# Router logits as 16 more columns of the mixing product, and expert choices ahead of the second norm of groups 1 and 2, in a one-core Perceiver layer

## The chip, the core and the metric

The kernel runs on one core of a Trainium2 chip. A core has five engines with queues of their own: PE (TensorE, matmul), DVE (VectorE), ACT (ScalarE), POOL (GpSimd) and SP (SyncE, which here issues DMAs only). Each engine works through its own list in order and waits on semaphores that the others raise. The metric is device time in microseconds of one execution, the median of several runs. All data are fp32 except where the text says otherwise; an fp32 matmul of 128 columns appears in the trace as two PE instructions.

## What is computed

32 batches of 32 query rows with 128 features (1024 tokens) pass through three residual blocks. Cut to what matters:

```python
x = x + xattn(layernorm(x), ctx, ctx, ...)            # 16 heads of 8, 257 keys per batch
# second block, u = layernorm(x), per batch of 32 rows
xf = concat([u[:, :1], u[:, 1:] @ WB.T]); xb = concat([u[:, 1:] @ WBf.T, u[:, -1:]])
gamma = sigmoid(xf @ w1.T + xb @ w2.T + b)            # one number per token
x = x + gamma * (xf + xb) + (1 - gamma) * u
# third block, v = layernorm(x): 8 experts, 2 per token
weights, chosen = top_k(v @ gate_kernel, 2); weights = softmax(weights)
x = x + sum over the 2 chosen of weight * ((silu(v @ w0[e]) * (v @ w1[e])) @ wo[e])
```

## The kernel before

Tokens stand on partitions in NT = 8 tiles of 128, and in three groups of tiles: group 0 is tiles 0 to 2, group 1 tiles 3 to 5, group 2 tiles 6 and 7 (`GROUPS`). There are three stages.

**Attention** is a loop over the 32 batches. Per batch PE makes keys and values (L843, L845), scores (L864), transposed probabilities (L876) and the weighted values (`weigh_values`, L905); DVE takes the row maxima, ACT the exponentials. In the batches 1 to 12 a query step of a later tile stands ahead of L905 (`late_step`, L899 and L902), and DVE's `take_output` drains it. POOL adds the heads of each batch (`add_heads`).

**The tail and the mix.** The output projection (`output_product`) and `add_residual` give x1. For each group: `row_sums` and `variances` on DVE (bn_stats, bn_aggr), an inverse root and a shift on POOL (`inverse_roots`), a normalisation on ACT (groups 0 and 1) or DVE (group 2), PE's transposes (`turn`), the shifted copies z, first and end (`shifted_features`), and then `mix`, with four matmuls per tile: z times `mix_sb[0]`, z one row on times `mix_sb[1]`, the first rows times w1, the last rows times an identity. Their output has D + 1 = 129 columns: 128 for the mixed rows less u, and one for the argument of gamma. The two vectors for that column of `mix_sb` come from `mix_vectors` (L920, L921) at the end of the attention loop. `gates` on ACT makes gamma; `mixed_rows` on DVE makes x2 = gamma * mixed + (u + x1).

**The experts.** x2 is normalised again by the same steps (`normalise(2, ...)`), transposed, and multiplied by the gate kernel (`logits`, L947). DVE's `best` and `best_at` find the two best of 8 per token; `pick` and `chosen` (L1419, L1422) are one-hots of them. PE counts the tokens of each expert and ranks them (L1017 to L1023). The rows are sent to `table` in DRAM by SP (L389, after the weights of both choices are in, `top_w_ready`), and 23 slots of 128 rows, each of one expert, are gathered back from it by POOL (`gather`, L590), transposed (`turn_slots`, L1069), and run through the expert (`half_hidden`, L1082; `project`, L1093). The first two slots (experts 0 and 1) don't wait for the table: one-hot matrices `late_at` are made on POOL, ACT and DVE from `early_rank`, and PE multiplies the normalised rows by them (`early_product`, L1031). `name_slots` (L1061) finds the row numbers for the gathers; `slot_row` (L1489) is what POOL waits for. ACT loads its Silu table (L735) after the weights.

The order is written out by hand in every engine's block. `keep_clock_up` (L805) is a matmul whose result nobody reads; it stands once ahead of the first turn and twice between the turns and the logits. `keep_sum` (L1009) moves x2 into two banks for the final sum.

Of the kernel before, what the change touches and what calls it, by code (L numbers as in the profile page):

```python
# [45 lines left out]
NT = TOK // 128  # L46
# [27 lines left out]
FAR = 4096  # L74

# [6 lines left out]
def build(nc, x, ctx_keys, ctx_last, weights, mix_back, vectors, rows, gate, w01, wo, out):  # L82
    with ExitStack() as stack:
# [3 lines left out]
        def sem(name):  # L87
# [50 lines left out]
        mix_sb = sb("mix_sb", [128, 2, D + 1])  # L138
        end_sb = sb("end_sb", [128, D + 1])
        u_x1 = sb("u_x1", [128, NT, D])  # L140
        gamma = sb("gamma", [128, NT])
# [57 lines left out]
        planes = nc.dram_tensor("planes", (TOPK * TOK, D), F32).ap()  # L199
        table = nc.dram_tensor("table", (TABLE_ROWS + 1, ROW), F32).ap()  # L200
# [52 lines left out]
        normed, norm_turned, norm_ft_ready, z_ready, edges_ready = (  # L253
            [sem(f"{name}{g}") for g in range(len(GROUPS))]
            for name in ("normed", "norm_turned", "norm_ft_ready", "z_ready", "edges_ready"))
        kl_done, kl_ready, wo_done = sem("kl_done"), sem("kl_ready"), sem("wo_done")
        mix_in, mix_ready, vectors_done, mixed_done, gamma_ready, u_x1_ready = (
            sem(n) for n in ("mix_in", "mix_ready", "vectors_done", "mixed_done", "gamma_ready", "u_x1_ready"))
        last_rows_ready = sem("last_rows_ready")
        logits_done, top_ready, top_w_ready, chosen_ready, ranks_done = (  # L260
            sem(n) for n in ("logits_done", "top_ready", "top_w_ready", "chosen_ready", "ranks_done"))
# [4 lines left out]
        first_gather_in, empty_stored = sem("first_gather_in"), sem("empty_stored")  # L266
        early_rank_ready, apart_ready = (sem(n) for n in ("early_rank_ready", "apart_ready"))
        pool_at_ready, act_at_ready = ([sem(f"{name}{n}") for n in range(EARLY)] for name in ("pool_at_ready", "act_at_ready"))
        dve_at_ready = sem("dve_at_ready")
# [38 lines left out]
        turn1_bank, turn2_bank = (bank[0], bank[1], bank[4]), (bank[3], bank[0], bank[1])  # L308
        logits_bank = (bank[2], bank[3], bank[0])
        ranks = bank[7][:, 192:192 + NT * E]  # L310
# [5 lines left out]
        def mixed(g, t):  # L316

            return mixed_bank[g][:, (D + 1) * t:(D + 1) * (t + 1)]
# [20 lines left out]
        def _(sp):  # L339
# [10 lines left out]
            sp.dma_start(table[TABLE_ROWS:TABLE_ROWS + 1, :], empty_row[0:1, :]).then_inc(empty_stored, 16)  # L350
            sp.wait_ge(zero_ready, 1)
# [31 lines left out]
            for g in range(len(GROUPS)):  # L383
                for c in range(TOPK):
                    if c == 1:
# [20 lines left out]
        def _(pool):  # L406
# [8 lines left out]
            def inverse_roots(nth):  # L415

                for g in range(len(GROUPS)):
                    t = group_tiles(g)
                    pool.wait_ge(var_ready, len(GROUPS) * (nth - 1) + g + 1)
                    if g < len(GROUPS) - 1:  # L420
                        own(pool.tensor_tensor(rstd[:, t], var_eps[:, t], minus_half[:, t], ALU.pow))
                        pool.tensor_tensor(shift[:, t], minus_mean[:, t], rstd[:, t], ALU.mult).then_inc(shift_ready, 1)
                    else:
                        pool.tensor_tensor(rstd[:, t], var_eps[:, t], minus_half[:, t], ALU.pow).then_inc(rstd_ready, 1)
# [30 lines left out]
            def expert_constants():  # L455
# [22 lines left out]
                pool.iota(no_row[:], [[0, 1]], base=TABLE_ROWS, channel_multiplier=0).then_inc(consts_ready, 1)  # L478
# [5 lines left out]
                pool.memset(ones[:], 1.0).then_inc(consts_ready, 1)  # L484
                own(pool.memset(before[:], 1.0))
# [6 lines left out]
            def mix_constants(m):  # L492

                if m == 0:
                    pool.memset(z_ft[:], 0.0).then_inc(mix_ready, 1)
# [5 lines left out]
                else:  # L501
                    pool.memset(end_ft[:], 0.0)
                    pool.tensor_copy(mix_sb[:, 1, 0:D], w_sb[:, W_BF]).then_inc(mix_ready, 1)

# [50 lines left out]
            for b in range(B + 2):  # L555
# [6 lines left out]
                if b >= 2:  # L562
                    add_heads(b - 2)
# [4 lines left out]
                if b % BPT == 2 and 2 <= b // BPT < 5:  # L568
                    mix_constants(b // BPT - 2)
# [3 lines left out]
            inverse_roots(1)  # L573
# [6 lines left out]
            inverse_roots(2)  # L580

            pool.wait_ge(normed[2], 2)
            for g in range(len(GROUPS)):
                t = group_tiles(g)
                pool.wait_ge(normed[g], 2)
                pool.tensor_copy(rows_tok[:, t, 1, 0:D], rows_tok[:, t, 0, 0:D]).then_inc(twin_ready, 1)
# [6 lines left out]


            pool.wait_ge(consts_ready, 13)
            pool.wait_ge(empty_stored, 16)
            pool.indirect_dma_start(slot_sb[SLOT_BUFS - 1][:], None, table, bass.IndirectOffsetOnAxis(no_row[:], 0)
                                    ).then_inc(first_gather_in, 16)

            pool.wait_ge(early_rank_ready, 1)  # L600
            for s in range(EARLY):
                for t in range(HT if s == 0 else 1):
                    pool.tensor_scalar(late_at[s][:, t, :], far_slot_nos[:], early_rank[:, t, s:s + 1], None, ALU.is_equal
                                       ).then_inc(pool_at_ready[s], 1)
# [3 lines left out]
            pool.wait_ge(first_gather_in, 16)  # L608
            for s in (2, 0, 3, 1, 4, 5):
# [23 lines left out]
        def _(act):  # L633
# [17 lines left out]
            def gates(g):  # L651

                act.wait_ge(mixed_done, g + 1)
                columns = mixed_bank[g][:, 0:(D + 1) * len(group(g))].rearrange("p (t c) -> p t c", c=D + 1)[:, :, D]
                act.activation(gamma[:, group_tiles(g)], columns, ACT.Sigmoid, bias=vec_sb[:, V_B]).then_inc(gamma_ready, 1)

            def features(g):

                act.wait_ge(norm_turned[g], 2)
                act.activation(norm_ft[:, group_tokens(g)], turn2_bank[g][:, group_columns(g)], ACT.Copy  # L660
                               ).then_inc(norm_ft_ready[g], 1)

# [61 lines left out]
            features(0)  # L724
            normalise(2, 1, x2_tok, rows_tok[:, :, 0, 0:D])
            features(1)

            for g in range(len(GROUPS)):
                act.wait_ge(top_ready, g + 1)
                for c in range(TOPK):  # L730
                    act.activation(rows_tok[:, group_tiles(g), c, D], top_d[:, group_tiles(g)], ACT.Sigmoid,
                                   scale=1.0 - 2.0 * c).then_inc(top_w_ready, 1)


            act.activation(table_loader[:], minus_half[:, 0:1], ACT.Silu)  # L735

# [5 lines left out]
            def early_at(s, t):  # L742

                act.wait_ge(apart_ready, HT * s + t - HT + 1)
# [3 lines left out]
            def early_one_hots(s):  # L748

                early_apart(s, HT)  # L750
                for t in range(HT, NT):
# [30 lines left out]
            early_one_hots(0)  # L782
            slot_features(0)
            early_one_hots(1)
# [15 lines left out]
        def _(pe):  # L800
# [87 lines left out]
            def weigh_values(b):  # L888
# [11 lines left out]
                elif step == "queries":  # L900
                    pe.wait_ge(late_ft_ready, i - LATE_TILES[0] + 1)
                    pe.matmul(o_bank[:, 384:512], w_sb[:, W_Q], norm_ft[:, tile(i)], start=True, stop=True)  # L902
                for g in range(G):
# [13 lines left out]
            def mix_vectors():  # L917

                pe.wait_ge(mix_in, 16)
                pe.matmul(bank[6][:, 384:385], mix_back_sb[:, 0, :], vec_sb[:, V_W1], start=True, stop=True)  # L920
# [680 lines left out]
```

## Time and profile before

| | us |
|---|---|
| median of 3 runs (lowest, highest) | 221.71 (221.41, 222.21) |
| the profiled execution | 223.38 |
| its span, first to last instruction | 221.6 |
| busy: PE, DVE, ACT, POOL | 207.0, 151.0, 139.1, 125.4 |
| granted TensorE clock, mean | 0.994 |

The granted clock is told as a share of full speed; its two levels are 2.4 GHz (1.0) and 1.2 GHz (0.5). The profile's chain of waits follows the work that ended last back from release to release; PE holds 79% of it, DVE 7%. In time it has three parts: up to about 113 us the attention loop, to about 141 us the tail, the mix, the second norm and the choices, and from there the 23 slots.

### The profile page before, as it was taken

Reading aid. Unit: us, or ns where it says so; the run is one execution under the profiler, and the core shown is the slowest. Engines: PE = TensorE matmul, PEld = TensorE weight load, DVE = VectorE, ACT = ScalarE, POOL = GpSimd, SP = SyncE. Lnnn points to the kernel's source line nnn. Section 1 sums busy time; section 2 is a strip of 40 time slices with the busy share of each in tenths; the row PEclk is TensorE's granted clock in tenths of the full one; section 3 lists DMA queues with packets and bytes.
Section 4 is the critical chain, followed back from the end, with each engine's and each line's share of the span. In section 5 each row is a group of like instructions: output and inputs, shape, how many; then the busy total and the mean of one; then the engine's idle time right before and its main releaser. Section 6 shows DMA issues by size and latency. Waiting matters only on the chain.

```text
span 221.6 us, 6244 instructions
## 1 busy us (share of the span) xinstructions
PE 207.0 (93%) x2069; PEld 176.3 (80%) x2069; DVE 151.0 (68%) x508; ACT 139.1 (63%) x436; POOL 125.4 (57%) x229
## 2 busy tenths in 40 slices
PE   6989999999999999999997889799999999999981
PEld 6866877887877777777775686589999999999970
DVE  3598887888787786878767577874445565655812
ACT  2158988988888988998895635753224444444300
POOL 2695575556675464353225547527777777775322
PEclk9999999999999999999999999999999999999997
DMA  6868406052160670000000001802122211122053
GB/s 185 304 211 304 154 19 237 10 173 78 30 224 15 220 215 12 7 12 4 13 5 3 3 0 52 158 11 50 51 54 56 48 42 46 38 44 40 6 189 95
DMA packets 14865, 18.93 MB, mean 85 GB/s; under 512 B 3039, under 2 KB 10467, under 8 KB 14834
## 3 DMA queue, kind: packets, MB, share of 16 engines
q1 hardware_dynamic: 12962, 15.35, 21.6%
q0 software_dynamic: 1440, 2.65, 5.8%
q10 hardware_dynamic: 432, 0.54, 0.7%
q8 instruction: 17, 0.28, 0.5%
q14 instruction: 14, 0.11, 0.2%
HBM read 14.73 MB, written 4.13 MB: 85 GB/s over the span
## 4 chain that ended last, share of the span: by engine, by line
PE 79%; DVE 7%; DMA 4%; POOL 3%; ACT 2%; issue 2%; POOLq 1%; SPq 1%; DVEq 0%; ACTq 0%
PE bank L1082 18%; PE bank L876 12%; PE bank L864 9%; PE bank L843 9%; PE bank L1093 8%; PE bank L905 8%; PE bank L845 6%; PE bank L1031 2%; DMA pt_sb<-planes 2%; DMA x_tok<-x 2%; DVE neg_max L1254 1%; PE bank L1069 1%; DMA planes<-y_sb,y_row 1%; POOL u_x L579 1%; PE bank L805 1%
## 5 line engine op out<-in xcount | busy, mean ns | idle before, releaser
L695 ACT ACTIVATE p_sb<-bank,neg_max 128x257 f32<-128x257 f32 x128 | 59.0, 473 | 15.3 <-DVE neg_max L1254 15.3
L1254 DVE TENSOR_REDUCE neg_max<-bank 128x1 f32<-128x257 f32 x128 | 46.0, 417 | 6.2 <-PE bank L864 5.7
L537 POOL TENSOR_TENSOR o_half<-o_masked 128x64 f32<-128x64 f32 x32 | 10.2, 318 | 45.8 <-DVE o_masked L1279 45.8
L704 ACT ACTIVATE pt_sb<-bank 128x512 f32<-128x512 f32 x64 | 35.0, 611 | 0.3 <-PE bank L876 0.3
L876 PE MATMUL bank<-ident,p_sb 128*128 128x128 f32 x256 | 33.3, 273 | 0.2 <-ACT pt_sb L704 0.2
L1082 PE MATMUL bank<-slot_ft,w_now 128*128 128x128 f32 x240 | 30.9, 276 | 0.0
L1551 DVE TENSOR_TENSOR hid_ft<-silu_sb,bank 128x512 f32<-128x512 f32 x23 | 15.8, 688 | 20.2 <-PE bank L1082 13.0
L876 PEld LDWEIGHTS bank<-ident,p_sb 128*128 128x128 f32 x256 | 28.9, 141 | 0.7 <-issue 0.7
L1082 PEld LDWEIGHTS bank<-slot_ft,w_now 128*128 128x128 f32 x240 | 29.1, 192 | 0.1
L590 POOL DMA_INDIRECT slot_sb<-table,slot_row x23 | 22.6, 984 | 10.7 <-issue 9.2
L616 POOL DMA_INDIRECT planes<-y_sb,y_row x21 | 22.2, 1059 | 10.5 <-DVE y_sb L1532 5.0
L771 ACT ACTIVATE slot_ft<-bank 128x128 f32<-128x128 f32 x23 | 6.4, 277 | 33.0 <-PE bank L1069 30.5
L695 ACT ACTIVATION_READ_ACCUMULATOR p_sb<-bank,neg_max 128x1 f32 x128 | 25.9, 203 | 0.0
L864 PE MATMUL bank<-kv_sb,qbd_sb 32*128 32x257 f32 x256 | 24.1, 429 | 1.3 <-DVE kv_sb L1264 1.3
L1093 PE MATMUL bank<-wo_sb,hid_ft 128*128 (+1 forms) x184 | 24.3, 275 | 0.0
L843 PE MATMUL bank<-ctx_sb,w_sb 128*128 128x256 f32 x64 | 22.7, 437 | 0.0
L1093 PEld LDWEIGHTS bank<-wo_sb,hid_ft 128*128 128x128 f32 x184 | 22.4, 192 | 0.0
L905 PE MATMUL bank<-pt_sb,kv_sb 128*32 128x128 f32 x512 | 21.3, 279 | 0.0
L845 PEld LDWEIGHTS bank<-w_sb,ctx_sb 128*128 128x128 f32 x128 | 19.8, 196 | 1.8
L1264 DVE TENSOR_TENSOR kv_sb<-bank,kv_bias 128x512 f32<-128x512 f32 x31 | 21.1, 682 | 0.0
L845 PE MATMUL bank<-w_sb,ctx_sb 128*128 128x128 f32 x128 | 19.9, 279 | 0.0
L516 POOL TENSOR_TENSOR ctx_sb<-ctx_sb,last_sb 128x256 f32<-128x256 f32 x31 | 18.9, 614 | 0.1
(219 smaller groups left out, 337.7 us busy)
## 6 DMA issues: line engine op xcount, KB each, us to landing
w_sb<-w SPq DMA_DIRECT2D x8, 512.0 KB, 4.8
ctx_sb<-ctx_keys SPq DMA_DIRECT2D x7, 512.0 KB, 4.1
wo_sb<-wo SPq DMA_DIRECT2D x8, 256.0 KB, 5.1
planes<-zero_rows SPq DMA_DIRECT2D x2, 512.0 KB, 6.6
pt_sb<-planes SPq DMA_DIRECT2D x4, 256.0 KB, 3.6
table<-rows_tok SPq DMA_DIRECT2D x4, 195.0 KB, 4.2
out<-norm_tok SPq DMA_DIRECT2D x2, 256.0 KB, 2.3
x_tok<-x SPq DMA_DIRECT2D x1, 448.0 KB, 5.0
```

The lines of the kernel that those rows point to most:

```text
L590: pool.indirect_dma_start(slot_sb[s % SLOT_BUFS][:], None, table, bass.IndirectOffsetOnAxis(slot_row[:, s:s + 1], 0)).then_inc(slot_in[s % ...
L616: pool.indirect_dma_start(planes, bass.IndirectOffsetOnAxis(y_row[s % Y_BUFS][:], 0), y_sb[s % Y_BUFS][:], None, bounds_check=last_row, oo ...
L695: act.activation(p_sb[b % 2][:, g, :], s_bank[g][:, 0:SKV], ACT.Exp, bias=neg_max[b % 2][:, g:g + 1], accum_out=sums[:, b, g:g + 1]).then_ ...
L704: act.activation(pt_sb[b % 2][:, t, :], pt_bank[t][:], ACT.Copy).then_inc((pt0_ready, pt1_ready)[t], 1)
L843: pe.matmul(kv_bank[:, 0:KEYS], w_sb[:, W_K], ctx[:, k, :], start=True, stop=True)
L845: last = pe.matmul(kv_bank[:, KEYS + 128 * t:KEYS + 128 * (t + 1)], ctx[:, k, tile(t)], w_sb[:, W_V], start=True, stop=True)
L864: pe.matmul(s_bank[g][:, 0:SKV], qbd_sb[b // BPT % 2][rows, b % BPT, :, :].rearrange("p j q -> p (j q)"), kv_sb[b % KV_BUFS][rows, 0, :], ...
L876: last = pe.transpose(pt_bank[t][:, tile(g)], p_sb[b % 2][:, g, tile(t)], ident[:])
L905: last = pe.matmul(o_bank[SQ * g:SQ * (g + 1), 0:128], kv_sb[b % KV_BUFS][:, 1, 128 * t + SQ * g:128 * t + SQ * (g + 1)], pt_sb[b % 2][:, ...
L1082: last = pe.matmul(bank[2 * m + s % 2][:, tile(c)], weights_now[:, tile(c)], slot_ft[s % 2][:], start=True, stop=True)
L1093: last = pe.matmul(bank[5][:, 0:D], hid_ft[s % 2][:, c, :], rows, start=(c == 0), stop=(c == FC - 1))
L1254: dve.tensor_reduce(neg_max[b % 2][:, g:g + 1], s_bank[g][:, 0:SKV], AX.X, ALU.max, negate=True).then_inc(max_ready, 1)
```

## The change

The mixing product gets 16 more columns (`COLS` = 145), from which the router's logits follow without the second norm's rows. The gate kernel less its column means, `centred`, is made once: PE multiplies the gate kernel by a matrix of 1/128 in batch 14 of the attention loop, DVE subtracts. In batch 18 PE multiplies WB and WBf by `gate_w` (the gamma vector beside `centred`), which replaces `mix_vectors`; POOL fills the constant parts in batch 22 (`mix_constants(3)`). Of the 16 columns 8 carry the logits of xf + xb - u and 8 those of u; DVE's `best` multiplies them by gamma and by 1 + std (`coef`; `deviations` on POOL), adds the two, and takes the best 8. Since the second norm's scale is one positive number per token, the choice needs no scale; `scale_tops` on POOL multiplies the difference of the two best by rstd before ACT makes the weights. Gone are `mix_vectors`, `features`, `logits`, the second `turn` and all three `keep_clock_up`.

```diff
-            keep_clock_up(1, bank[5])
             turn(1, 0, norm_tok, turn1_bank[0])
             pe.wait_ge(mix_ready, 5)
+            pe.wait_ge(vectors_ready, 1)
             mix(0, range(0, 2))
...
-            turn(2, 0, rows, turn2_bank[0])
...
+            pe.wait_ge(x2_ready, 2)
             keep_sum(0)
-            keep_sum(1)
             pe.wait_ge(chosen_ready, 1)
...
+            pe.wait_ge(x2_ready, 3)
+            keep_sum(1)
...
+                pe.wait_ge(normed[0], 2)
+                pe.wait_ge(normed[1], 2)
+                pe.wait_ge(dve_at_ready[0], 1)
+                for t in range(2, HT + 1):
+                    early_product(0, t, t == 2, False)
...
+                elif b == CENTRED_AT:
...
+                    pe.matmul(o_bank[:, 384:384 + E], mean_mat[:], gate_sb[:], start=True, stop=True)
+                elif b == VECTORS_AT:
...
+                        pe.matmul(o_bank[:, 384 + 16 * m:384 + 16 * m + 1 + E], mix_back_sb[:, m, :], gate_w[:, m, :],
+                                  start=True, stop=True)
...
+                own(dve.tensor_tensor(logit_parts[:, t, :, :],
+                                      mixed_tiles(g)[:, :, D + 1:COLS].rearrange("p t (k e) -> p t k e", e=E),
+                                      coef[:, t, :].unsqueeze(3).to_broadcast(by_part), ALU.mult))
+                own(dve.tensor_tensor(router[:, t, :], logit_parts[:, t, 0, :], logit_parts[:, t, 1, :], ALU.add))
...
+            best(0)
+            mixed_rows(0)
+            row_sums(0, x2_tok)
             best_at(0)
-            features(2)
+            variances(0)
             best(1)
+            mixed_rows(1)
+            best_at(1)
             best(2)
...
+            mixed_rows(2)
+            row_sums(1, x2_tok)
...
+            early_one_hots(0, 2)
+            variances(1)
+            row_sums(2, x2_tok)
+            variances(2)
```

Other moves: the last batch's heads are added on DVE in one reduction (`add_last_heads`) instead of on POOL, and `variances(0)` of the first norm stands ahead of the last `take_output`; `variances(1)` stands ahead of `add_residual(2)`. On POOL the first indirect DMA (a dummy gather, now from a table of its own, `first_table`) stands ahead of the second norm's roots, and the copies of the rows for choice 1 (`twin`) of groups 1 and 2 stand behind all one-hots. SP sends the rows of choice 0 after `normed` and those of choice 1 after `twin`. ACT makes the weights of groups 1 and 2 and loads the Silu table behind the one-hots.

On DVE, before, the choices end the second norm's list (`bank3` and `bank0` hold the logits of groups 1 and 2):

```order
L1188 COPY norm_ft<-bank1 128x256 [waits norm_turned2]
L1393 MAX top<-bank3 128x8 [waits logits_done]
L1393 MAX top<-bank3 128x8 x2
L1395 TENSOR_TENSOR top_d<-top 128x3 [waits dve_step]
L1393 MAX top<-bank0 128x8 [waits logits_done]
L1393 MAX top<-bank0 128x8
L1395 TENSOR_TENSOR top_d<-top 128x2 [waits dve_step]
L1401 MAX_INDEX top_at<-top,bank3 128x8 x3
L1401 MAX_INDEX top_at<-top,bank0 128x8 x2
L1419 TENSOR_TENSOR pick<-expert_no,top_at 128x64 [waits consts_ready,dve_step]
L1419 TENSOR_TENSOR pick<-expert_no,top_at 128x64
L1422 TENSOR_TENSOR chosen<-pick 128x64 [waits dve_step]
```

Now, from the choices of group 2 on, the x2 rows of group 2 and the statistics of group 1 come behind `chosen`:

```order
L1457 MAX_INDEX top_at<-top,router 128x8 [waits tops_ready]
L1457 MAX_INDEX top_at<-top,router 128x8
L1473 TENSOR_TENSOR pick<-expert_no,top_at 128x64 [waits consts_ready,dve_step]
L1473 TENSOR_TENSOR pick<-expert_no,top_at 128x64
L1476 TENSOR_TENSOR chosen<-pick 128x64 [waits dve_step]
L1392 SCALAR_TENSOR_TENSOR x2_tok<-bank7,coef,u_x1 128x128 [waits u_x1_ready,gamma_ready]
L1392 SCALAR_TENSOR_TENSOR x2_tok<-bank7,coef,u_x1 128x128
L1195 BN_STATS stats<-x2_tok 128x6 [waits x2_ready]
L1195 BN_STATS stats<-x2_tok 128x6 x2
L1500 SCALAR_TENSOR_TENSOR early_rank<-chosen,bank5 128x16 [waits ranks_done]
L1486 TENSOR_TENSOR z_ft<-far_slot_nos,early_rank 128x384 [waits early_rank_ready]
L1203 BN_AGGR mean_var<-stats 128x2 [waits dve_step]
```

So the choice no longer waits for any normalised row, and the variance of group 1 waits for the choice. On PE, before, the ranks are followed by the early products, which wait only for one-hots:

```order
L1023 MATMUL bank7<-chosen,ones 128x16
L1023 MATMUL bank7<-chosen,ones 128x8
L1031 MATMUL bank3<-z_ft,rows_tok 128x128 [waits pool_at_ready0,expert_in]
L1031 MATMUL bank3<-z_ft,rows_tok 128x128 [waits act_at_ready0]
L1031 MATMUL bank3<-z_ft,rows_tok 128x128 [waits pool_at_ready0]
```

Now the second half of x2 is moved behind the ranks, and the early products wait for normalised rows too:

```order
L1055 MATMUL bank5<-chosen,ones 128x16
L1055 MATMUL bank5<-chosen,ones 128x8
L1041 MATMUL bank6<-x2_tok,ident 128x512 [waits x2_ready]
L1065 MATMUL bank3<-z_ft,rows_tok 128x128 [waits normed1,dve_at_ready0,normed0,expert_in]
L1065 MATMUL bank3<-z_ft,rows_tok 128x128 x2
L1065 MATMUL bank3<-z_ft,rows_tok 128x128 [waits pool_at_ready0]
L1065 MATMUL bank3<-z_ft,rows_tok 128x128 [waits act_at_ready0]
```

Between the mix and `normed1` PE is left with two moves of x2 and the ranks.

## Rows read from the trace of the kernel before

**Rows 1.** Chain of waits, attention: start us, us, engine, line, instructions.

```profile
60.34 0.22 PE bank L902 x2
```

**Rows 2.** Timeline of PE, last batch: start us, us, engine, line, work [idle before].

```profile
116.16 1.06 PE L876 MATMUL bank<-ident,p_sb 128*128 128x128 f32 x8 [0.17 <-ACT pt_sb L704]
```

**Rows 3.** Timeline, first norm of group 0 on DVE, POOL and ACT.

```profile
118.13 0.67 DVE L1153 BATCH_NORM_STATS2 stats<-x_tok 128x6 f32<-128x128 f32 x3
...
120.35 0.89 POOL L421 TENSOR_TENSOR rstd<-var_eps,minus_half 128x3 f32<-128x3 f32 x1
...
121.55 1.26 ACT L638 ACTIVATE norm_tok<-x_tok,shift,rstd 128x128 f32<-128x128 f32 x3 [2.12 <-POOL shift L422]
```

**Rows 4.** Timeline of PE, the mix; each tile starts with L932.

```profile
124.07 0.68 PE L932 MATMUL bank<-mix_sb,z_ft 128*128 128x129 f32 x4 [0.66 <-ACT z_ft L647]
...
127.37 0.61 PE L932 MATMUL bank<-mix_sb,z_ft 128*128 128x129 f32 x4
...
128.27 0.61 PE L932 MATMUL bank<-mix_sb,z_ft 128*128 128x129 f32 x4
```

**Rows 5.** Chain of waits, second norm of group 0.

```profile
127.87 0.88 DVE x_tok L1337 x3
...
128.77 0.69 DVE stats L1153 x3
...
129.49 0.32 DVE mean_var L1161 x3
...
130.15 0.87 POOL rstd L421
...
131.32 1.27 ACT rows_tok L638 x3
```

**Rows 6.** Chain of waits, choices, and early products of slot tile 1.

```profile
138.22 0.81 DVE top_at L1401 x6
...
139.45 0.23 DVE chosen L1422
...
146.67 1.90 PE bank L1031 x16
```

**Rows 7.** Timeline of PE, early products of slot tile 0.

```profile
141.38 2.48 PE L1031 MATMUL bank<-z_ft,rows_tok 128*128 128x128 f32 x16 [1.09 <-POOL z_ft L603]
```

**Rows 8.** Timeline of DVE: in the list of ranks, and behind it.

```profile
141.06 0.21 DVE L1445 TENSOR_TENSOR square<-n_tiles,expert_before 128x64 f32<-128x64 f32 x1
...
145.89 0.54 DVE L1485 TENSOR_TENSOR late_at<-far_slot_nos,early_rank 128x384 f32<-128x384 f32 x1
```

**Rows 9.** Timeline of POOL, its one-hots of slot tile 0.

```profile
140.62 2.48 POOL L603 TENSOR_SCALAR z_ft<-far_slot_nos,early_rank 128x128 f32<-128x128 f32 x4 [2.03 <-DVE early_rank L1435]
```

**Rows 10.** Timeline of ACT, Silu table and first steps of its one-hots.

```profile
138.66 1.28 ACT L735 ACT_TABLE_LOAD   x1
...
140.60 0.69 ACT L739 ACTIVATE z_ft<-far_slot_nos,early_rank 128x128 f32<-128x128 f32 x2 [0.44 <-DVE early_rank L1435]
```

**Rows 11.** Timeline of POOL, the first gather.

```profile
147.66 1.04 POOL L590 DMA_INDIRECT slot_sb<-table,slot_row  x1 [3.98 <-issue]
```

**Rows 12.** Chain of waits, PE takes slot 2.

```profile
150.97 0.11 PE bank L1069
```

**Rows 13.** DMA issues, 130 to 160 us: KB each, median us from issue to landing.

```profile
table<-rows_tok SPq DMA_DIRECT2D x2, 130.0 KB, 5.7
slot_sb<-table,slot_row POOLq DMA_INDIRECT x8, 2.5
```

**Rows 14.** Timeline of PE at the start of the span.

```profile
1.75 4.64 PE L817 MATMUL bank<-ident 128*128 128x128 f32 x20 [1.75 <-POOL ident L445]
...
9.65 1.06 PE L817 MATMUL bank<-ident 128*128 128x128 f32 x4
```

**Rows 15.** Timeline of PE, its last work.

```profile
214.66 2.02 PE L1103 MATMUL bank<-y_sb,late_at 128*128 128x128 f32 x16 [0.54 <-DVE y_sb L1532]
```

**Rows 16.** Busy by window: window, length, PE, PEld, DVE, ACT, POOL busy, PEclk, DMA.

```profile
219.00:219.50 0.50, 0.00 (x0) 0.00 (x0) 0.00 (x0) 0.00 (x0) 0.00 (x0) 0.60 0.26 76
```

More of the change, by code:

```diff
@@ L571, in _ @@
                     residual(2 * (b // BPT - 2) + b % BPT // 3)
-            inverse_roots(1)
+            for g in range(len(GROUPS)):
+                inverse_root(1, g)
+            deviations()
             pool.wait_ge(normed[2], 1)
@@ L653, in gates, with top_weights @@
                 act.wait_ge(mixed_done, g + 1)
[L654 to L661, printed above, removed]
+                act.activation(coef[:, group_tiles(g), 0], mixed_tiles(g)[:, :, D], ACT.Sigmoid, bias=vec_sb[:, V_B]
+                               ).then_inc(gamma_ready, 1)
+            def top_weights(g):
+                act.wait_ge(top_ready, g + 1)
+                for c in range(TOPK):
+                    act.activation(rows_tok[:, group_tiles(g), c, D], top_d[:, group_tiles(g)], ACT.Sigmoid,
+                                   scale=1.0 - 2.0 * c).then_inc(top_w_ready, 1)
             act.dma_start(w_sb[:], weights).then_inc(w_in, 16)
@@ L723, in _ @@
             gates(2)
[L724 to L735, printed above, removed]
+            top_weights(0)
             def early_apart(s, t):
@@ L781, in _ @@
             act.wait_ge(early_rank_ready, 1)
-            early_one_hots(0)
+            early_one_hots(0, HT + 1)
+            normalise(2, 1, x2_tok, rows_tok[:, :, 0, 0:D])
+            top_weights(1)
+            top_weights(2)
             slot_features(0)
-            early_one_hots(1)
+            early_one_hots(1, HT)
+            act.activation(table_loader[:], minus_half[:, 0:1], ACT.Silu)
             gate_silu(0)
@@ L941, in mix @@
                     last.then_inc(mixed_done, 1)
-            def logits(g):
-                pe.wait_ge(norm_ft_ready[g], 1)
-                for n, t in enumerate(group(g)):
-                    last = pe.matmul(logits_bank[g][:, E * n:E * (n + 1)], norm_ft[:, tile(t)], gate_sb[:],
-                                     start=True, stop=True)
-                last.then_inc(logits_done, 1)
             pe.wait_ge(consts_ready, 1)
@@ L1016, in _ @@
             for t in range(NT):
-                last = pe.matmul(bank[7][:, 128:128 + E], ones[:], chosen[:, t, :], start=(t == 0),
+                last = pe.matmul(counts, ones[:], chosen[:, t, :], start=(t == 0),
                                  stop=(t == NT - 1))
@@ L1336, in mixed_rows @@
                 for n, t in enumerate(group(g)):
[L1337 removed]
+                    last = dve.scalar_tensor_tensor(out=x2_tok[:, t, :], in0=mixed(g, n)[:, 0:D], scalar=coef[:, t, 0:1],
                                                     in1=u_x1[:, t, :], op0=ALU.mult, op1=ALU.add)
```

243 lines of the change are left out of this document (148 added, 95 removed).

## The prediction

> **What bounds the kernel now.** I read four views in this order. The chain of waits shows which engine has no slack where. In the attention loop it is PE alone, piece behind piece without a gap: even a query product that one batch more or less carries stands on the chain with its full 0.22 us [rows 1]. From about 113 us on, the chain changes engine every half microsecond: norm, mix, norm again, choices. From the early products at 141.38 on [rows 7] it is PE again, to the end. The timelines of the single engines then show what each wait is for, the DMA issues when the table is readable, and the windows the granted clock. So three things can be gained or lost: PE work in the loop, the length of the path from the last batch to the early products, and the level of PE's clock. All positions below are on the scale of the trace of before, whose span is 221.6 us; the program's own time was 223.38, so 1.8 lie around the span and stay. I add the differences to the median, 221.71.
>
> **Attention: +0.6.** Three small products join PE's list in batches 14 and 18. As the loop has no gap, each counts. The row shows 0.22 for one of 128 columns [rows 1]; these have 8 or 9 columns but load as many weights, so I take 0.2 each, 0.6, with 0.3 and 0.66 as ends. The two products that they replace stood where PE waited for ACT's copy anyway, 0.17 idle even with them in front [rows 2]: their removal gives nothing.
>
> **First norm: -0.9.** The row sums of group 0 end at 118.80, yet POOL begins the root at 120.35 only [rows 3]: the statistics stood behind the last drain, and POOL behind the last heads. Now the statistics follow the sums at once. From first aggregate to root takes 0.66 (129.49 to 130.15 [rows 5]), so the root can start at 119.46, 0.9 earlier. ACT's normalisation, PE's turn and the mix start (124.07 [rows 4]) follow by the same 0.9, since the unread 512-column product ahead of that turn is gone as well. Adding the last heads on DVE costs one reduction there and saves two POOL steps: nothing net. I keep -0.7 to -1.0.
>
> **Mix: +0.08 a tile.** A tile takes 0.90 (127.37 to 128.27 [rows 4]) for four matmuls, three of them 129 columns wide, so some 0.224 per matmul. 16 columns more are an eighth: 0.028 for each of the wide three, nothing for the fourth, which goes from 1 to 17. That makes 0.08 a tile, between 0 and 0.11. Group 0 is mixed 0.65 earlier (three tiles), all eight 0.25 earlier, at about 131.7.
>
> **Choices: 4.6 earlier.** DVE takes group 0 at 127.87 - 0.65 = 127.2. `best(0)` is two small dependent steps, as `chosen` 0.23 each, and three maxima, as the index steps 0.135 each (0.81 for six [rows 6]): 0.86. Then x2 0.88, sums 0.69 [rows 5], indices 0.41, statistics 0.66: POOL's root starts at 130.7, 0.55 later than before. It is 1.17 from there to ACT (130.15 to 131.32) and 1.27 through it [rows 5]: 133.15. The gate of group 2 stands behind that in ACT's queue, another quarter microsecond by estimate from the small steps: 133.4. `best(2)` 0.73, two indices 0.27, and 0.65 for `pick` and `chosen` (139.03 to 139.68 [rows 6]) give `chosen` at 135.05, against 139.68.
>
> **Second norm: most of that is given back.** The early products now wait for the normalised rows of group 1, and these for statistics behind `chosen` on DVE: x2 of group 2 (0.59), sums (0.69), rank 0.2, one-hots 0.54 [rows 8], statistics 0.66 put POOL's root at 137.75; 1.17 and 1.27 more, and a handover of 0.1, put the first product at 140.3. Before: 141.38 [rows 7]. So 1.1 is left of 4.6. The products themselves took 2.48 there, since they waited for POOL's and ACT's one-hots; with these ready they take 1.90, as those of slot tile 1 do [rows 6]. End: 142.2 instead of 143.87, 1.7 earlier. Behind them DVE's list limits: sums and statistics of group 2 end it at 138.75, then the 5.4 from early rank to 145.89 [rows 8] and 0.6 for normalising group 2, so 144.75, 1.15 earlier; PE needs only the second half of it there, and comes out 1.5 to 1.6 earlier at slot tile 1. POOL's one-hot for the sixth product (0.62 [rows 9]) ends 0.5 before its turn. The Silu load, 1.28 and once hidden, now stands behind eight one-hot steps of 0.3 [rows 10] and ahead of `slot_features(1)`; ACT gets free 0.1 to 0.2 before it is needed. I price that at 0, up to 0.5. Total of the path: **-1.5**.
>
> **Gathers: 0.** Slot 2 was gathered from 147.66 [rows 11], landed 2.5 later [rows 13] and was taken at 150.97 [rows 12]: 0.8 of slack. `slot_row` moves by about as much as PE. The last table rows go out at about 142.5 now, behind two one-hots and two row copies on POOL; before, the last two needed 5.7 [rows 13], with six stores close together and the dummy gather among them. Four stand together now and the gather is far ahead; I take 3 and no cost.
>
> **The clock: +1.6.** This term decides the sign. Between the end of the mix (131.7) and the first early product (140.3) PE has two moves of x2 of 0.9 each and the ranks, 0.6: 2.4 us of work in 8.6. The second move starts when x2 of group 2 is there, at 135.65, and ends at 136.55; then PE has nothing for 3.7 us. The unread products that stood in this stretch are gone. In the trace of before the longest pause of PE between the loop and the end of the slots is the 1.09 us ahead of these products [rows 7], and the granted clock is full there. It falls once: PE's last work ends at 216.68 [rows 15], the window from 219.0 reads 0.60 [rows 16], so the clock went from 2.4 to 1.2 GHz at about 219.1, after 2.4 us without work. An idle stretch of 3.7 us, behind a thin one, is more of the same. What the lower level costs is seen at the start: 20 instructions of 128 columns in 4.64 [rows 14] are 0.44 per product with the last one's tail off, against 0.24 [rows 6], so 0.2 more each. If the eight early products run at it, that is **1.6**. Nearest below is 0 (no fall). Above, the start shows PE still at the lower level in the products at 9.65 [rows 14], 8 us after its first work; at the same pace here `half_hidden(0)` with its eight matmuls would pay another 1.6, and the next early products some more. I take the eight products, the value between.
>
> **Sum.** 221.71 + 0.6 - 1.5 + 1.6 = **222.4**, slower by 0.3%, which is also about the smallest difference that a measurement of this kernel can tell from none.
>
> **Rivals.** *The clock stays high* (chance 0.30): same sum without the last term, 220.8, so 0.4% faster. For it: the stretch isn't empty, and the moves of x2 are the densest work there. Against it: 3.7 us of nothing. It decides by whether PE's clock falls before 140.3. *The clock stays low for longer, or falls a second time* (0.20): after the last batch PE has, without the first unread product, only about 1 us of work between 119.7 and 123.1; if the clock is low in the mix too, or through `half_hidden(0)`, another 1.6 is paid: 224.0. *The table lands late* (0.08): with 5.7 again the last rows land at 148.2, the gather starts then and lands at 150.7, while PE wants slot 2 at 149.5, so 1.2 to 2 lost, 222 to 222.8 with a high clock. A rule speaks for this one: the Trainium skill, SBUF — State Buffer, § Who interferes with whom, says that GpSimd and a VectorE operation with two SBUF inputs lock each other out for a whole instruction, and `twin` of groups 1 and 2 now runs beside DVE's long one-hots. The row beside it speaks against: DVE's two-input step at 141.06 took its 0.21 [rows 8] in the middle of POOL's four one-hots at 0.62 each [rows 9]. By the rule the stores would leave a microsecond later, by the row at once. *The change doesn't do what it says* is not left: the choices wait for no normalised row in the new order; what can fail is only that their lead is worth little, which the sum has in it.
>
> **How the numbers follow.** Forecast 0.42, clock high 0.30, clock low for longer 0.20, late table 0.08. The limits of 0.3% are 221.05 and 222.37. Faster: three quarters of the high clock, 0.24 with a rest. Same: what is left of it, nearly half of the forecast, a part of the late table: 0.28. Slower: 0.48. The range has to hold the high clock at -0.3 for the uncertain terms, 220.5, and the long fall, 224.1.
>
> **What would show it.** Right: a PEclk under 1 between 137 and 146 us of the new trace, early products of over 0.3 per product, `chosen` at about 135.7 (0.6 later on the new scale), first early product near 140.9, batches 14 and 18 longer by 0.2 and 0.4. Wrong: a clock of 1 throughout; PE waiting for slot 2; ACT's table load ahead of `slot_features(1)` on the chain; PE idle for less than 3 us ahead of the early products.

## The result, and the profile after

The changed kernel takes **224.79 us** (median of 20 runs, 222.19 to 227.07) where the kernel before took 221.50 in the same comparison (20 runs, 220.67 to 222.21): ratio 1.013, 95% interval 1.011 to 1.015, so 3.3 us slower. Medians are of all runs; ratios and intervals, here and below, leave out runs over 1.5% above the fastest of their kernel, three of the twenty here. The forecast had the sign, but only 0.7 us of it (222.4 on its base of 221.71), and the time lies above its range, which ended at 224.1.

First a correction to the scale. The trace of before took 223.38 us, 1.9 over its median, and the difference lies wholly at its start, which the change doesn't touch: by their durations PE's first products ran at the lower level until past 10 us [rows 14]. Another trace of the kernel before (run e10 below, 221.96 us) has an early start, as that of after has, and everything behind it stands 1.9 us earlier than in the rows ahead of the prediction. Rows of after are therefore compared with those of e10. From PE's timeline in e10 (start, duration, line, in brackets the idle time before and who ended it):

```profile
11.94 1.06 PE L864 MATMUL bank<-kv_sb,qbd_sb 32*128 32x257 f32 x8 [0.88 <-DVE kv_sb L1264]
...
114.25 1.06 PE L876 MATMUL bank<-ident,p_sb 128*128 128x128 f32 x8 [0.17 <-ACT pt_sb L704]
...
119.81 1.02 PE L805 MATMUL bank<-w_sb,ident 128*128 128x512 f32 x2
...
122.16 0.68 PE L932 MATMUL bank<-mix_sb,z_ft 128*128 128x129 f32 x4 [0.66 <-ACT z_ft L647]
...
139.47 2.48 PE L1031 MATMUL bank<-z_ft,rows_tok 128*128 128x128 f32 x16 [1.09 <-POOL z_ft L603]
...
147.00 2.05 PE L1082 MATMUL bank<-slot_ft,w_sb 128*128 128x128 f32 x16 [0.37 <-ACT slot_ft L771]
148.89 0.27 PE L1069 MATMUL bank<-ident,slot_sb 128*128 128x128 f32 x1
...
212.77 2.02 PE L1103 MATMUL bank<-y_sb,late_at 128*128 128x128 f32 x16 [0.54 <-DVE y_sb L1532]
```

The same timeline of after (the rows answer to [rows 2, 4, 6, 7, 12, 15]):

```profile
11.88 1.07 PE L914 MATMUL bank<-kv_sb,qbd_sb 32*128 32x257 f32 x8 [0.88 <-DVE kv_sb L1301]
...
114.67 1.06 PE L926 MATMUL bank<-ident,p_sb 128*128 128x128 f32 x8 [0.62 <-ACT pt_sb L762]
...
119.79 0.71 PE L975 MATMUL bank<-w_sb,att_ft 128*128 128x128 f32 x4 [1.13 <-DVE att_ft L1366]
120.51 0.78 PE L861 MATMUL bank<-ident,norm_tok 128*128 128x128 f32 x3
121.95 1.30 PE L986 MATMUL bank<-mix_sb,z_ft 128*128 128x145 f32 x4 [0.66 <-ACT z_ft L705]
...
123.96 1.17 PE L986 MATMUL bank<-mix_sb,z_ft 128*128 128x145 f32 x4
...
128.17 0.66 PE L986 MATMUL bank<-mix_sb,z_ft 128*128 128x145 f32 x4
...
129.14 0.66 PE L986 MATMUL bank<-mix_sb,z_ft 128*128 128x145 f32 x4
...
136.35 0.35 PE L1049 MATMUL bank<-chosen,ones 128*128 128x8 bf16 x8 [1.93 <-DVE chosen L1476]
...
136.86 1.23 PE L1041 MATMUL bank<-x_tok,ident 128*128 128x512 f32 x2
141.50 3.49 PE L1065 MATMUL bank<-z_ft,rows_tok 128*128 128x128 f32 x16 [3.41 <-ACT rows_tok L696]
...
150.05 2.05 PE L1124 MATMUL bank<-slot_ft,w_sb 128*128 128x128 f32 x16 [0.37 <-ACT slot_ft L817]
151.94 0.27 PE L1111 MATMUL bank<-ident,slot_sb 128*128 128x128 f32 x1
...
216.07 2.02 PE L1145 MATMUL bank<-y_sb,late_at 128*128 128x128 f32 x16 [0.54 <-DVE y_sb L1601]
```

The mix begins 0.2 earlier than in e10, yet its first tile takes 2.01 (121.95 to 123.96) where a later one takes 0.97 (128.17 to 129.14), and the early products take 3.49. The windows of after say why (the last number but two is the granted clock):

```profile
120.00:122.00 2.00, 1.33 (x8) 0.77 (x7) 1.86 (x12) 1.09 (x5) 0.89 (x2) 0.67 0.00 0
122.00:124.00 2.00, 2.00 (x9) 2.00 (x10) 0.85 (x5) 1.26 (x3) 1.62 (x5) 0.50 0.00 0
124.00:126.00 2.00, 2.00 (x10) 1.99 (x10) 0.00 (x0) 0.00 (x0) 2.00 (x3) 0.50 0.00 0
126.00:128.00 2.00, 2.00 (x13) 2.00 (x12) 0.57 (x3) 0.64 (x3) 1.67 (x2) 0.62 0.00 0
128.00:130.00 2.00, 2.00 (x18) 2.00 (x19) 1.26 (x8) 0.26 (x1) 0.00 (x0) 1.00 0.31 33
...
136.00:138.00 2.00, 1.65 (x18) 0.77 (x18) 1.90 (x9) 0.04 (x1) 0.29 (x1) 0.94 0.50 149
138.00:140.00 2.00, 0.09 (x1) 0.00 (x0) 1.90 (x15) 1.84 (x7) 1.80 (x4) 0.50 0.01 4
140.00:142.00 2.00, 0.50 (x2) 0.53 (x3) 1.94 (x13) 1.75 (x7) 1.84 (x6) 0.50 0.00 0
142.00:144.00 2.00, 2.00 (x12) 2.00 (x11) 1.97 (x7) 0.00 (x0) 2.00 (x4) 0.50 0.33 100
144.00:146.00 2.00, 1.63 (x11) 1.44 (x11) 2.00 (x3) 0.97 (x4) 0.93 (x1) 0.85 0.65 186
```

PE's clock falls to 1.2 GHz twice: from about 120.7 to 127.5 us, under the mix of group 0, and from about 137.8 to 144.6, under the early products. The forecast had the second fall alone, and read it from the pause of 3.41 us ahead of the early products. The rows put it earlier: at 137.8 PE is still at the second move of x2 (136.86 to 138.09), behind a pause of 1.93, and the long pause has not begun.

### The profile page after: what moved, and what is told of

It is laid out like the page before. It is cut to its first block, busy times and chain, and to the rows that moved or that the text cites. A ratio compares the mean times of both kernels' runs of the same rounds, so it can differ in the third digit from the quotient of the medians.

```text
span 223.0 us, 6218 instructions
## 1 busy us (share of the span) xinstructions
PE 204.0 (92%) x2041; PEld 175.4 (79%) x2041; DVE 151.9 (68%) x515; ACT 137.5 (62%) x432; POOL 127.6 (57%) x243
## 4 chain that ended last, share of the span: by engine, by line
PE 78%; DVE 9%; DMA 4%; ACT 3%; issue 2%; POOL 1%; POOLq 1%; SPq 1%; DVEq 0%; ACTq 0%
PE bank L1124 17%; PE bank L926 12%; PE bank L914 9%; PE bank L893 8%; PE bank L966 8%; PE bank L1135 8%; PE bank L895 6%; PE bank L1065 2%; DMA pt_sb<-planes 2%; DMA x_tok<-x 2%; PE bank L986 1%; DVE neg_max L1291 1%; ACT rows_tok L696 1%; PE bank L1111 1%; DMA planes<-y_sb,y_row 1%
## 5 line engine op out<-in xcount | busy, mean ns | idle before, releaser
L674 POOL DMA_INDIRECT planes<-y_sb,y_row x21 | 21.6, 1030 | 11.3 <-DVE y_sb L1601 5.9
L895 PEld LDWEIGHTS bank<-w_sb,ctx_sb 128*128 128x128 f32 x128 | 19.3, 191 | 1.7
L895 PE MATMUL bank<-w_sb,ctx_sb 128*128 128x128 f32 x128 | 19.4, 274 | 0.0
```

The lines of the kernel that those rows point to most:

```text
L674: pool.indirect_dma_start(planes, bass.IndirectOffsetOnAxis(y_row[s % Y_BUFS][:], 0), y_sb[s % Y_BUFS][:], None, bounds_check=last_row, oo ...
L895: last = pe.matmul(kv_bank[:, KEYS + 128 * t:KEYS + 128 * (t + 1)], ctx[:, k, tile(t)], w_sb[:, W_V], start=True, stop=True)
```

## The experiments

The theory drawn from these rows: the path gets shorter as forecast, and two falls of the clock eat that and more. The rivals: the longer mix and the new order themselves cost; the table comes late. Each run has its median, its lowest and highest time, and the ratio to the kernel before, timed beside it (221.67 for e1 to e4, 221.57 for e5 to e7), with a 95% interval.

**e1, the mix filled.** One unread product is put back, in a place where PE waits anyway.

```diff
             spread_last()
+            keep_clock_up(1, bank[5])
             output_product(2)
```

> The changed kernel (224.8 us, median of its runs) with one product that nobody reads put back, between `spread_last()` and `output_product(2)`, where PE sat idle for 1.13 us. Clock theory: the change's loss comes from two stretches in which PE's granted clock is 0.50, the first from about 121 to 127 us of the changed kernel, in the mix of group 0, because the unread product that stood ahead of that mix is gone. In that stretch the two turns and the three mix tiles of group 0 took about 3.0 us more than at the upper level (tiles of 2.01, 1.88 and 1.26 us against 0.97, turns of 0.78 and 1.07 against 0.55). So the clock stays up there, PEclk 1.00 from 118 to 134, and the time falls by 2 to 3 us, to 221.8 to 222.8. Rival, the path theory: the mix waits on VectorE and ScalarE anyway and the loss is the longer work itself (145 columns instead of 129, choices on DVE): then the time falls by 0.3 us at most, 224.5 or more.

Measured: 223.99 (222.33 to 224.38), ratio 1.010, 1.008 to 1.012. The trace is of its fastest run; PE's timeline:

```profile
121.65 0.73 PE L986 MATMUL bank<-mix_sb,z_ft 128*128 128x145 f32 x4 [0.66 <-ACT z_ft L705]
...
138.78 3.76 PE L1066 MATMUL bank<-z_ft,rows_tok 128*128 128x128 f32 x16 [3.51 <-ACT rows_tok L696]
...
149.49 0.27 PE L1112 MATMUL bank<-ident,slot_sb 128*128 128x128 f32 x1
```

The mix is at the upper level and the first early product comes 2.7 us earlier than in after (138.78 against 141.50). PE ends 2.4 earlier (215.72 against 218.09). Of the 2 to 3 us expected, the median gives only 0.8; the other runs come back below, at e9.

**e2, the gap filled.** Four unread products, one behind the first move of x2, three behind the second.

```diff
             keep_sum(0)
+            keep_clock_up(1, bank[0])
...
             keep_sum(1)
+            keep_clock_up(3, bank[0])
```

> The changed kernel with four unread products in PE's second thin stretch: one behind `keep_sum(0)`, three behind `keep_sum(1)`, into a bank that is free there; PE sat idle there for 1.93 and 3.41 us. Clock theory: the fall from about 137.8 to 144.6 goes, the sixteen early product instructions of slot 0 take 1.9 to 2.0 us instead of 3.49, and the time falls by about 1.5 us, to about 223.3; the first fall, in the mix, stays. Path theory: the early products wait on the second norm and on the one-hots, the time falls by 0.3 at most, 224.5 or more, or rises by what the three products (3.1 us in a gap of 3.4) push.

Measured: 223.99 (222.47 to 226.22), ratio 1.010, 1.006 to 1.013. In its trace the early products are down to 2.02, and a wait stands in PE's timeline that after did not have:

```profile
139.02 2.02 PE L1067 MATMUL bank<-z_ft,rows_tok 128*128 128x128 f32 x16 [0.93 <-ACT rows_tok L696]
...
149.73 0.33 PE L1113 MATMUL bank<-ident,slot_sb 128*128 128x128 f32 x1 [1.49 <-DMA slot_sb<-table,slot_row]
```

In this execution the clock stayed up in the mix too, without a product there: that fall doesn't come every time. Of the 1.5 us expected, the median gives 0.8; the new wait takes 1.49 in the trace. On POOL, the last two row copies (`twin`) and the gather of slot 2:

```profile
140.62 1.84 POOL L462 COPY rows_tok<-rows_tok 128x384 f32<-128x384 f32 x2
147.02 1.11 POOL L636 DMA_INDIRECT slot_sb<-table,slot_row  x1 [4.57 <-DMA table<-rows_tok]
```

**e3, both.**

> Both fillings together. Clock theory: both falls go and the two gains add, 3.0 + 1.5 us: 220.0 to 221.0, below the kernel before (221.5), since the path of the change itself (forecast: 1.5 us off the path, 0.6 or less on the attention) then shows. Path theory: 224 or more. If the two falls are one thing (the second comes only because the first has moved the rest), the sum is less than that of the two alone.

Measured: 222.80 (222.54 to 223.11), ratio 1.005, 1.003 to 1.007. So 2.0 of the 3.3 us come back with the clock, and the spread of 4.9 us (20 runs) shrinks to 0.6 (5 runs); but the kernel is still 1.1 slower than before, where the clock theory alone said 0.5 to 1.5 faster. PE's timeline shows the reason, POOL's and DVE's what is behind it:

```profile
138.98 2.02 PE L1068 MATMUL bank<-z_ft,rows_tok 128*128 128x128 f32 x16 [0.94 <-ACT rows_tok L696]
...
149.90 0.33 PE L1114 MATMUL bank<-ident,slot_sb 128*128 128x128 f32 x1 [1.79 <-DMA slot_sb<-table,slot_row]
```

```profile
140.69 2.91 POOL L462 COPY rows_tok<-rows_tok 128x384 f32<-128x384 f32 x2
147.16 1.11 POOL L636 DMA_INDIRECT slot_sb<-table,slot_row  x1 [3.56 <-DMA table<-rows_tok]
```

```profile
140.69 2.65 DVE L1555 TENSOR_TENSOR at_slot<-slot_nos,slot_in_tile 128x1024 f16<-128x1024 f16 x2
```

The two row copies (`twin`) begin in the same moment as DVE's `at_slot` and take 2.91; the last table rows leave behind them, and the gather waits for those rows. The length of the copies is not all of it: in e2 they end 1.1 us earlier (142.46 against 143.60), yet the gather starts only 0.14 earlier, since 4.57 us lie between the two instead of 3.56. Why is not shown; the slowest of the six issues of these rows took 0.97 in e2, 0.44 in e3 and 1.48 in e5 below.

**e4, the kernel before without its first unread product.**

```diff
             output_product(2)
-            keep_clock_up(1, bank[5])
 
             turn(1, 0, norm_tok, turn1_bank[0])
```

> The kernel before without its first unread product (ahead of the turn of group 0); the other two unread products stay, nothing else changes. Clock theory: this product alone kept the clock up in the mix of group 0, so the clock falls to 0.50 there as in the changed kernel, and the time rises by 2 to 3 us, to 223.5 to 224.5. Rival, that other things in the change (the shorter first norm, the wait on the vectors, the longer pause of 1.13 us ahead of the last output product) make the fall: the clock stays up and the time stays at 221.5 or falls by up to 0.2, the part of the product that stood in front of the turn.

Measured: 224.28 (223.43 to 224.41), ratio 1.012, 1.010 to 1.014. Two windows of its trace:

```profile
122.00:124.00 2.00, 1.90 (x11) 1.93 (x12) 0.78 (x4) 1.37 (x5) 1.21 (x4) 0.63 0.02 8
124.00:126.00 2.00, 2.00 (x11) 2.00 (x11) 0.05 (x1) 0.00 (x0) 2.00 (x3) 0.52 0.00 0
```

This one line is worth 2.6 us of the kernel before: without it the clock falls in the mix, as in after. The longer mix and the new order are not needed for that fall. The trace is of the fastest of the four runs and has 1.6 of the 2.6 us (the second half of slot 1 at 148.58 against 147.00 in e10); the mean granted clock of the three slower runs is lower, 0.978 to 0.984 against 0.992, so they spent more time at the lower level, but where is in no trace.

**e5, the table earlier.** As e3, and on POOL:

```diff
             early_one_hot(0, 1)
-            early_one_hot(1, 0)
             twin(1)
             twin(2)
+            early_one_hot(1, 0)
```

> Both fillings of e3, and on POOL the two copies `twin(1)` and `twin(2)` ahead of the last one-hot, `early_one_hot(1, 0)`, instead of behind it. In the trace of e3 the clock is at its upper level to the last slot, and yet the kernel takes 222.8 against 221.7 of the kernel before; PE waits 1.79 us for the gather of slot 2, which waits for the table, whose last rows wait for these two copies: they took 2.91 us for the two beside DVE's two long `at_slot` steps (140.69 to 143.60), against 1.30 for three in the kernel before. Table theory: ahead of `at_slot` they take 0.4 to 0.5 each, the last rows leave about 2.5 us earlier, the gather no longer makes PE wait, and the time falls by 1.5 to 1.8 us, to 221.0 to 221.3. Rival: the copies are slow whatever stands beside them, or the landing of the rows (3.3 us) is what counts: then 222.5 or more.

Measured: 221.37 (12 runs, 220.93 to 221.97) against 221.57 for the kernel before, ratio 0.9995, 0.998 to 1.001, just above the 221.0 to 221.3 expected. POOL's timeline, then PE's:

```profile
139.06 0.61 POOL L642 TENSOR_SCALAR z_ft<-far_slot_nos,early_rank 128x128 f32<-128x128 f32 x1
139.63 1.11 POOL L462 COPY rows_tok<-rows_tok 128x384 f32<-128x384 f32 x2
140.72 1.80 POOL L642 TENSOR_SCALAR late_at<-far_slot_nos,early_rank 128x128 f32<-128x128 f32 x1
145.53 1.11 POOL L636 DMA_INDIRECT slot_sb<-table,slot_row  x1 [3.01 <-DMA table<-rows_tok]
```

```profile
148.21 0.33 PE L1114 MATMUL bank<-ident,slot_sb 128*128 128x128 f32 x1
```

The copies take 0.55 each, and now the one-hot that stands beside `at_slot` (140.92 to 143.36 here) takes 1.80 instead of 0.61. Slot 2 is taken 1.7 earlier than in e3, and the time is 1.4 less: the late table was the rest of the loss. It still isn't early. The copies end 2.9 earlier than in e3 (140.74 against 143.60), but the gather starts only 1.6 earlier, 4.79 us behind them, when the last rows have landed. PE takes 9.99 from the second half of slot 1 to slot 5 (146.04 to 156.03) where e7 takes 9.36 (146.30 to 155.66); two waits for gathered rows, 0.6 together, stand in there. These 0.6 eat most of the 0.9 that the path gives. At PE's end 0.07 is left (214.72 against 214.79 in e10), and the 0.2 between the medians is within the interval.

**e6, the order on POOL alone**, the edit of e5 without any filling.

> The changed kernel with the order of POOL's steps of e5 alone, no filling. Clock theory with the table behind it: PE's two falls make PE later than the table (slot 2 was taken without a wait there), so the earlier table gives nothing: 224.8, within 0.5. Rival, that the late table is the main loss of the changed kernel and the clock a side effect: 223.3 or less.

Measured: 223.98 (222.36 to 226.39), ratio 1.009, 1.006 to 1.013. This median lies below the clock theory's band (224.3 at least) and above the rival's (223.3 at most). But two of the six runs are over 226, the median of the other four is 223.3, at the rival's bound, and the intervals of e6 and after overlap: inconclusive. Whether the earlier table gives something while the clock falls stays open. Its trace, the fastest run, happens to have no fall in the mix, and the clock low from about 133 to 143.3.

**e7, the first norm alone.** The kernel before with that part of the change, and its first unread product moved in front of `output_product(2)`.

```diff
             spread_last()
+            keep_clock_up(1, bank[5])
             output_product(2)
-            keep_clock_up(1, bank[5])
...
                     row_sums(0, x1_tok)
+                    variances(0)
...
-            variances(0)
+            add_last_heads()
+            add_residual(1)
             scale_keys(NT - 1)
```

> The kernel before with the first part of the change alone: the statistics of group 0 directly behind its sums, the last heads added on DVE by one reduction, POOL free of them; the choices, the second norm and the last two unread products as before, and the first unread product moved between `spread_last()` and `output_product(2)`, where PE waits anyway. Forecast's step: 0.9 us off the path, at the mix and, since all behind it is one chain to the early products, at the end: 220.6 to 220.9. Rival, that the gain is given back at the second norm (ACT's normalisation of group 1 or DVE's queue sets the choices): 221.3 or more.

Measured: **220.83** (12 runs, 220.14 to 221.78), ratio 0.997, 0.996 to 0.999: 0.7 faster than before, of the 0.9 forecast for this part, and the fastest of all versions here. POOL's root starts at 117.52 against 118.45 in e10; PE's timeline has the gain still at slot 2 (148.89 in e10):

```profile
138.75 2.48 PE L1031 MATMUL bank<-z_ft,rows_tok 128*128 128x128 f32 x16 [1.08 <-POOL z_ft L603]
...
148.19 0.27 PE L1069 MATMUL bank<-ident,slot_sb 128*128 128x128 f32 x1
```

**e8, the changed kernel again; e9, e1 again; e10, the kernel before again**, one run each.

> The changed kernel once more, for one more trace. Its times lie between 222.2 and 227.1 us, a spread of 4.9 against 1.5 of the kernel before. Clock theory: in another execution the stretches at the lower level have other places and lengths against the same work, and the time follows them; the work at the upper level has the same durations. Rival: something else varies (DMA landings, the start).

> e1 (the changed kernel with its unread product back in front of the mix) once more. Its five times lie between 222.3 and 224.4 us, and the trace of it is of the fastest. Clock theory: the mix is at the upper level here too (PEclk 1.00 from 118 to 131 on a start like e1's), and where the time is longer it is the second stretch at the lower level that lies on more work, early products and the halves of slot 0, than the 136.0 to 142.6 of e1. Rival: the filling doesn't hold the clock each time, and the mix is slow again.

> The kernel before once more. The trace shown of it took 223.38 us against a median of 221.5, and its attention loop begins 2 us later than that of the changed kernel, since PE's first products run at the lower level until 10 us instead of 6. Start theory: this is a matter of the single execution, so that this trace, if its time is near 221.5, shows the second batch's scores at about 11.9 instead of 13.55 and everything behind 2.0 us earlier, the first early product at 139.4 and slot 2 at 148.9. Rival: the change makes the start faster: then they are at 13.5, 141.4 and 150.8 again.

Measured: 227.38, 223.00 and 221.96. e8 has both falls (windows at 0.50 from 124 to 130 and from 142 to 146), and a late start besides: its last batch stands at 116.77 instead of 114.67, so 2.1 of its 2.6 us over the median are the start, as the rival had it. For the spread of the twenty timed runs the record speaks for the clock: their mean granted clock goes from 0.979 in the fastest (222.19) to 0.957 in the slowest (227.07), and by and large the time follows it. e9 again has the mix at the upper level and early products of 3.75. e10 has its second batch at 11.94 and slot 2 at 148.89, as the start theory said. What made four of e1's five runs 0.9 to 2.1 slower than the one traced was not seen; in both its traces the mix is at the upper level. More time at the lower level is not it for three of the four: their mean granted clock, 0.981 to 0.984, is above the 0.978 of the traced run. So the trace shows what the filling does to the path; why the median gives only 0.8 stays open.

Traces with an early start side by side (start in us, from PE's and DVE's timelines; the last two columns are the time of the traced execution and the median of the timed runs):

| kernel | last batch | mix | `chosen` | first early product | second half of slot 1 | slot 2 | PE ends | traced | median |
|---|---|---|---|---|---|---|---|---|---|
| before (e10) | 114.25 | 122.16 | 137.54 | 139.47 | 147.00 | 148.89 | 214.79 | 222.0 | 221.5 |
| after | 114.67 | 121.95 | 136.06 | 141.50 | 150.05 | 151.94 | 218.09 | 224.7 | 224.8 |
| e1 | 114.60 | 121.65 | 133.35 | 138.78 | 147.60 | 149.49 | 215.72 | 222.3 | 224.0 |
| e3 | 114.79 | 121.83 | 133.54 | 138.98 | 146.06 | 149.90 | 216.38 | 222.8 | 222.8 |
| e5 | 114.76 | 121.80 | 133.49 | 138.92 | 146.04 | 148.21 | 214.72 | 222.0 | 221.4 |
| e7 | 114.19 | 121.24 | 136.83 | 138.75 | 146.30 | 148.19 | 214.10 | 220.7 | 220.8 |

`chosen` in DVE's timelines of e10, after and e3:

```profile
137.54 0.23 DVE L1422 TENSOR_TENSOR chosen<-pick 128x64 bf16<-128x64 f32 x1
136.06 0.23 DVE L1476 TENSOR_TENSOR chosen<-pick 128x64 bf16<-128x64 f32 x1
133.54 0.22 DVE L1479 TENSOR_TENSOR chosen<-pick 128x64 bf16<-128x64 f32 x1
```

## Why the prediction was wrong, and what in it was right

**Attention, +0.6: right.** The last batch stands 0.42 later in after than in e10, 0.35 to 0.54 in e1, e3 and e5. From one batch's scores to the next, the interval with the first new product (64.84 in after) is 0.12 longer than in e10, the one with the other two (77.78) 0.35; 0.2 and 0.4 were forecast. The two products that went gave nothing: PE waits 0.62 for ACT ahead of the last batch instead of 0.17.

**First norm, -0.9: right.** Behind the last batch the mix starts 7.04 us later in e3 against 7.91 in e10. e7 brought that part alone, and it reached the end.

**Mix, +0.08 a tile: right.** 0.97 (128.17 to 129.14 in after) against 0.90 [rows 4].

**Choices and second norm: right, where the clock is up.** Forecast were `chosen` 4.6 and the first early product 1.1 earlier, and attention 0.6 later, so -4.0 and -0.5 in all; e3 has -4.0 and -0.5. At the second half of slot 1, -0.9 was forecast and e3 has -0.9. The table load of ACT didn't come onto the chain.

**The clock, +1.6: the step that failed.** The fall under the early products came and cost what was forecast: 3.49 instead of 2.02 in after, 1.5 us (1.7 in e1). That is in part luck, since the pause it was read from is not where the clock fell. The forecast hung the fall on 3.7 us of nothing ahead of these products, as more of the 2.4 us without work behind the last slot. In after the clock fell while the second move of x2 still ran, in e1, e8 and e9 0.4 to 0.8 us behind that move, and in e6 ahead of it, about 1.25 us into the pause of 1.93: in none of them after 2.4 us without work. And the step looked at this one stretch only. The unread product ahead of the first turn was counted as a hindrance, "gone as well", and its effect on the clock was left to a rival with a chance of 0.20 and a price of 1.6. e4 shows that the kernel before needs it: 2.6 us. In after this fall moves `chosen` from 133.54 (e3) to 136.06, 2.5 us. The sum with both is -0.9 + 2.5 + 1.5 = 3.1; PE is 3.05 later at the second half of slot 1 and 3.3 at its end. The rival named the place and the mechanism; its price was too low, because it counted a fall as eight products at the lower level: the fall in the mix covered two turns and three tiles, at 2.01, 1.88 and 1.26 instead of 0.97 each.

**Gathers, 0: wrong, and hidden by the error above.** The forecast let the last rows go out at 142.5, which is 141.2 on the scale of e3 (start 1.9 earlier, attention 0.6 later), and land in 3 us. In e3 the copies end at 143.60 and the gather starts 3.6 later, so that PE waits 1.79 for slot 2. Two terms were too small: the two copies took 2.91 beside `at_slot` (in e10 three take 1.30), and from the end of the copies to the gather it is 3.6 in e3, 4.6 in e2 and 4.8 in e5. With the copies moved away 1.4 us came back (e5). The rival of the late table had the place and the size, 1.2 to 2 lost at a high clock, with a chance of 0.08; it counted on a landing of 5.7, where in e3 the rows left 2.4 late and landed in 3.6. In the trace of after nothing of this shows: PE is late enough by its clock to find slot 2 there. Here the rule of the Trainium skill that the prediction set aside (SBUF — State Buffer, § Who interferes with whom: one of the two engines is blocked for a whole instruction of the other) agrees with the rows: whichever of copy or one-hot stands beside `at_slot` is stretched, the two copies of e3 to 1.39 and 1.57 from 0.4 to 0.5, the one-hot of e5 to 1.80 from 0.61. In after, where the copies began a hair earlier (143.09 against 143.11), the first of them kept its 0.50, the two steps of `at_slot` took 2.89 instead of 2.35, and the second copy 1.39. The row on which the rule was set aside was of a step of 0.21, not of one of 1.2. POOL and DVE in after:

```profile
143.09 1.84 POOL L462 COPY rows_tok<-rows_tok 128x384 f32<-128x384 f32 x2
143.11 2.89 DVE L1552 TENSOR_TENSOR at_slot<-slot_nos,slot_in_tile 128x1024 f16<-128x1024 f16 x2
```

**The rival "clock stays high", 220.8**, would have been about 222.8 as the change stands (e3), because of the table. So the forecast's sum would have been too low in either case.

## What to carry to other kernels

Before an unread product is removed from ahead of dense work, take it out alone and look at the granted clock: one line was worth 2.6 us here, more than the 0.9 us that the whole path of the change gained. Look at every stretch in which the change thins PE's list, not at the longest pause only, and price a fall by all the work under it. When such a loss is filled, expect the next wait behind it: here a copy on POOL that had met no long DVE step before the reordering, and met one after it, and a table that landed later than priced.

## What the hardware showed besides

The start of one and the same code differs between executions by 1.9 to 2.1 us, seen at the last batch (before against e10, e8 against after). By their durations PE's unread products from 1.75 on come to the upper level during the first twenty instructions or right behind them (e10: 4.34 us for the twenty, 0.61 for the next four, first scores at 9.16), or only behind those four (before: 4.64 and 1.06 [rows 14], first scores at 10.64). The windows give 1.00 there in both cases, so only the durations tell.

The fall in the mix came in three of five traces without an unread product ahead of it (after, e4, e8; not e2, e6), though PE's list there is the same in all but e4, and in none of the seven with one (both of before, e1, e3, e5, e7, e9). The longest pause ahead of it was 1.13 us, with an output product, a turn and 0.66 more of waiting behind it. What decides between a fall and none was not found. The fall ahead of the early products, with pauses of 1.92 or 1.93 and of 2.56 to 3.51 us, came in all five traces without a filling there (after, e1, e6, e8, e9) and in none of the seven with unread products there (both of before, e2 to e5, e7).
